# Copying the row numbers of a scatter before the waits for its data, in a mixture-of-experts kernel

## The chip, the cores and the metric
The kernel runs on 1 core of one Trainium2 chip. The metric is device time in microseconds (us) of one execution; smaller is better. Times inside a profile are counted from the first instruction of the profiled execution.

## The reference
Two residual stages over x, 4 x 512 tokens of 512 numbers. The first adds a gated mix of a sigmoid of two rank-one scores and the normalised x. The second adds a gated mixture of experts over the normalised result: every token goes through a shared expert and through its 4 best of 16 experts, with weights packed as 4-bit codes.
```
x = x + tanh(g_xattn) * (0.6 * sigmoid(si + sj + b) + 0.4 * layernorm(x))
h = layernorm(x)
probs = softmax(h @ gate_w.T);  vals, idx = top_k(probs, 4);  w = vals / sum(vals)
y_e = (silu(h @ G_e) * (h @ U_e)) @ D_e          # expert e, weights dequantised
out = sum over the 4 chosen e of w_e * y_e  +  shared expert(h)
x = x + tanh(g_ffn) * out
```

## The kernel before
**Stages.** The first stage, the gating and the shared expert over 16 tiles of 128 tokens come first. The normalised rows are stored to a DRAM table `token_rows`, and x with the shared expert's part is stored to `out`. From about 195 us on the routed part runs: the tokens of each expert are listed in slots of 128 (`tok` holds the row numbers, one column for a slot; short slots are filled with a dump row). In this data there are 72 slots, numbered 0 to 71, and each expert has one slot or more.

**One slot.** POOL (GpSimd) gathers the 128 rows by an indirect DMA into `xg` (line 504); PE transposes them (line 1236), does gate and up (line 1196, in two halves), transposes the activations (line 1210) and does the down product (line 1224); ACT and DVE do the work between. ACT copies the product to `y_sb` (line 640, `mix_room` in the rows) and raises `yev_done`. POOL then adds the 128 rows into `out` by an indirect DMA with an add (line 524), the scatter, and each landed scatter raises `added[b]` by 16. There are two buffers, b = 0 and 1, taken in turn. In slot s PE does the gate and up of s and the down product of s - 1. While that goes on, DVE dequantises the next expert's weights, which SP's queue loads.

**POOL's queue.** It holds, in program order, `gather(s + 4)` and `add(s)` for each slot. The last four adds (68 to 71) have no gathers between them, and are written out behind the loop. An indirect DMA takes its row numbers from a small tile: `idx_g` for gathers and `idx_s` for scatters, each with a column for each buffer, filled by a copy of one column of `tok`. `hold_wait()` (line 493, `pool_tick` in the rows) is a small multiply on POOL that carries the wait ahead of the DMA instruction.

**The waits of a scatter.** A read-add-write of the same row by two scatters must not overlap. Slots of one expert hold different tokens, slots of different experts may hold the same. `added[b] >= 8 * (s - b)` says that scatter s - 2, the last of this buffer, has landed. `others_i` holds for the first slot of an expert the count of `added[1 - b]` that says that all earlier scatters of the other buffer have landed, and 16 for all other slots; POOL's sequencer loads it into a register from SBUF (line 516). The last scatter waits for all before it (line 519). `st_out` says that the plain stores to `out` have landed (line 520).

Of the kernel before, what the change touches and what calls it, by code (L numbers as in the profile page):

```python
# [29 lines left out]
def gated_xattn_moe(nc, x, ctx_512, g_xattn, g_ffn, xattn_w, xattn_b, gate_w, gu_packed, gu_scales,  # L30
                    dn_packed, dn_scales, sh_gu_packed, sh_gu_scales, sh_dn_packed, sh_dn_scales, out):
    B, S, H = x.shape
# [32 lines left out]
    with ExitStack() as ctx:  # L65
        def sb(name, shape, dt):
            return ctx.enter_context(nc.sbuf_tensor(name, shape, dt))
# [4 lines left out]
        def sem(name):  # L72
            return ctx.enter_context(nc.semaphore(name))
# [87 lines left out]
        def in_room_b(shape, dt):  # L161

            n = math.prod(shape[1:])
            piece = room_b[:, at[0]:at[0] + n]
            at[0] += n
            assert at[0] <= B * S
            if dt != F32:
                piece = piece.bitcast(dt)
            return piece.rearrange("p (a b) -> p a b", a=shape[1]) if len(shape) == 3 else piece
        tok = in_room_b([P, SLOTS], I32)  # L170
# [35 lines left out]
        idx_s = sb("idx_s", [P, 2], I32)  # L206
# [64 lines left out]
        st_out = sem("st_out")  # L271
# [16 lines left out]
        yev_done = sem("yev_done")  # L288
        added = [sem("added0"), sem("added1")]
        idx_g_ready = sem("idx_g_ready")  # L290
        idx_s_ready = sem("idx_s_ready")
# [110 lines left out]
        def _(pool):  # L402
# [88 lines left out]
            def hold_wait():  # L491

                nc.gpsimd.tensor_tensor(pool_tick[:, :], ones[:, 0:1], ones[:, 0:1], ALU.mult)
# [12 lines left out]

            def add(s, b, all_before=False):

                pool.wait_ge(yev_done, s + 1)
                if not isinstance(s, int) or s >= 2:  # L510
                    pool.wait_ge(added[b], 8 * (s - b))
                if isinstance(s, int):
                    if s >= 1:
                        pool.wait_ge(added[1 - b], 8 * (s + b))
                else:
                    others = pool.value_load(others_i[0:1, bass.ds(s, 1)], min_val=16, max_val=8 * SLOTS)
                    pool.wait_ge(added[1 - b], others)
                if all_before:
                    pool.wait_ge(added[1 - b], 8 * (s + b))
                pool.wait_ge(st_out, 16 * (B + 1))  # L520
                nc.gpsimd.tensor_copy(idx_s[:, b:b + 1], tok[:, bass.ds(s, 1)]).then_inc(idx_s_ready, 1)  # L521
                pool.wait_ge(idx_s_ready, s + 1)
                hold_wait()
                nc.gpsimd.indirect_dma_start(out[:, :], bass.IndirectOffsetOnAxis(idx_s[:, b:b + 1], 0), y_sb[:, b, :],  # L524
                                             None, compute_op=ALU.add).then_inc(added[b], 16)
            for s in range(4):
                gather(s, s % 2)
            for b in range(2):
                gather(b + 4, b)
                add(b, b)  # L530
            with pool.Fori(2, inner + 1) as j:
                for b in range(2):
                    gather(2 * j + b + 2, b)
                    add(2 * j + b - 2, b)
            for k in range(-4, 0):
                add(2 * inner + 4 + k, k % 2, all_before=k == -1)
# [819 lines left out]
```

## Time and profile before
| | |
|---|---|
| time, median of 3 runs | 717.2 us (716.89 to 717.4) |
| profiled execution, its own time | 715.78 us |
| its span, first to last instruction | 714.1 us |
| mean granted TensorE clock | 0.953 of full speed |
| PE busy (matmul) | 87% of the span |
| DVE, ACT, POOL busy | 69%, 46%, 45% |

The engines are PE (TensorE matmul), PEld (its weight loads), DVE (VectorE), ACT (ScalarE), POOL (GpSimd) and SP (SyncE). An engine's name with a q (POOLq) is its instruction sequencer, which resolves waits and registers ahead of the engine. "Issue" is time in which an engine waited for nothing that the profile shows. A releaser is what ended an idle time; where an instruction had several waits, the one that came last is named.

### The profile page before, as it was taken

How to read it: one execution, taken by the hardware profiler on the slowest of the kernel's cores; microseconds unless marked ns; L12 is line 12 of the kernel's file. 1: busy time of each engine (PE TensorE's matmuls, PEld its weight loads, DVE VectorE, ACT ScalarE, POOL GpSimd, SP SyncE). 2: the span in 40 equal slices, each digit the busy share in tenths (PEclk: the TensorE clock that was granted, in tenths of full speed). 3: DMA queues.
4: the chain of work that ended last, by engine and by line, in shares of the span. 5: the costliest groups of instructions: out<-in, count | busy, mean ns of one | idle time of the engine just before them, and what ended most of it. 6: DMA issues, size and time to landing. Idle time of an engine off the chain costs nothing.

```text
span 714.1 us, 17257 instructions
## 1 busy us (share of the span) xinstructions
PE 620.8 (87%) x4394; PEld 374.8 (52%) x4395; DVE 490.2 (69%) x1271; ACT 325.8 (46%) x558; POOL 324.8 (45%) x506
## 2 busy tenths in 40 slices
PE   3347459995979899999999999999999999999991
PEld 2234236653545456656556566565565556566550
DVE  4695847889857576758778758578678787867110
ACT  1751347632234355455445455454554544554541
POOL 1620354200032456556465475554655646665532
PEclk9759788999899999999999999999999999999997
DMA  6940011204627668584785886758576686754532
GB/s 222 294 139 0 16 45 74 75 1 85 232 53 204 156 143 211 97 210 86 184 187 118 192 175 136 178 106 201 119 180 149 141 204 132 165 88 85 86 40 38
DMA packets 49841, 93.72 MB, mean 131 GB/s; under 512 B 8840, under 2 KB 16776, under 8 KB 49816
## 3 DMA queue, kind: packets, MB, share of 16 engines
q0 software_dynamic: 16128, 38.35, 28.8%
q1 hardware_dynamic: 29464, 49.83, 24.3%
q10 hardware_dynamic: 4224, 5.24, 2.2%
q8 instruction: 11, 0.18, 0.1%
q14 instruction: 14, 0.11, 0.1%
HBM read 65.16 MB, written 28.24 MB: 131 GB/s over the span
## 4 chain that ended last, share of the span: by engine, by line
PE 69%; DVE 13%; DMA 6%; issue 4%; SPq 2%; ACT 2%; POOL 1%; DVEq 1%; POOLq 0%; ACTq 0%
PE gu_ps L1196 41%; PE bank L1224 19%; PE bank L1236 4%; PE bank L1210 4%; DMA dn_sc<-dn_scale_halves 3%; DVE act L987 1%; DMA dn_scale_halves<-wgu 1%; ACT acth L616 1%; DVE stats L721 1%; DVE X L996 1%; DVE mix_room L1023 1%; DVE X L751 1%; PE bank L1180 1%; DVE acth L992 1%; DVE wgu L923 1%
## 5 line engine op out<-in xcount | busy, mean ns | idle before, releaser
L1196 PE MATMUL gu_ps<-wgu,mix_room 128*128 x1728 | 305.4, 327 | 2.4 <-DVE tick L946 1.3
L1196 PEld LDWEIGHTS gu_ps<-wgu,mix_room 128*128 128x128 f16 x1728 | 166.3, 98 | 114.3 <-issue 8.6
L1224 PE MATMUL bank<-wdn,aT 128*128 (+1 forms) x792 | 187.2, 382 | 12.1 <-ACT aT L623 11.5
L623 ACT ACTIVATE aT<-bank 128x768 f16<-128x768 f16 x88 | 71.2, 810 | 130.5 <-PE bank L1210 130.5
L524 POOL DMA_INDIRECT out<-mix_room,idx_s x72 | 121.6, 1689 | 18.5 <-issue 17.9
L1224 PEld LDWEIGHTS bank<-wdn,aT 128*128 128x128 f16 x792 | 77.7, 98 | 97.8 <-ACT aT L623 7.8
L987 DVE SCALAR_TENSOR_TENSOR act<-gu_ps,wslot,sg x72 | 44.5, 618 | 104.5 <-ACT sg L609 91.4
L616 ACT ACTIVATE acth<-act 128x384 f16<-128x384 f32 x88 | 46.0, 523 | 133.0 <-DVE act L987 128.3
L521 POOL COPY idx_s<-room_b 128x1 int32 (+1 forms) x72 | 19.0, 263 | 180.9 <-DMA out<-mix_room,idx_s 117.6
L501 POOL COPY idx_g<-room_b 128x1 int32 (+1 forms) x72 | 58.5, 813 | 75.7 <-DVE tick L857 62.6
L504 POOL DMA_INDIRECT room_b<-token_rows,idx_g x72 | 78.5, 1090 | 10.8 <-issue 1.0
L1196 PE MATMUL gu_ps<-wgu,xT 128*128 128x384 f16 x384 | 72.7, 344 | 5.6 <-DVE tick L980 5.6
L992 DVE TENSOR_TENSOR acth<-act,acth (+1 forms) x88 | 49.5, 563 | 39.6 <-ACT acth L616 38.4
L634 ACT ACTIVATE mix_room<-bank 128x1024 f16<-128x1024 f16 x72 | 73.2, 1017 | 0.5 <-PE bank L1236 0.5
L923 DVE TENSOR_TENSOR wgu<-dq_code,gu_sc 128x768 f16<-128x768 f16 x136 | 71.7, 569 | 2.4
L609 ACT ACTIVATE sg<-gu_ps 128x384 f32<-128x384 f32 x88 | 43.2, 491 | 65.6 <-PE gu_ps L1196 62.0
L1210 PE MATMUL bank<-id,acth 128*128 128x128 f16 x528 | 44.1, 220 | 13.3 <-ACT acth L616 9.3
L1196 PEld LDWEIGHTS gu_ps<-wgu,xT 128*128 128x128 f16 x384 | 38.0, 103 | 31.4 <-issue 11.5
L1210 PEld LDWEIGHTS bank<-id,acth 128*128 128x128 f16 x528 | 36.2, 98 | 27.5 <-ACT acth L616 16.6
L1236 PE MATMUL bank<-id,room_b 128*128 128x128 f16 x576 | 44.4, 220 | 2.8 <-DMA room_b<-token_rows,idx_g 2.8
L929 DVE TENSOR_TENSOR wdn<-dn_code,dn_sc 128x384 f16<-128x384 f16 x136 | 42.9, 357 | 0.7
L640 ACT ACTIVATE mix_room<-bank 128x512 f32<-128x512 f32 x72 | 41.8, 580 | 3.0 <-PE bank L1224 3.0
(161 smaller groups left out, 581.5 us busy)
## 6 DMA issues: line engine op xcount, KB each, us to landing
dn_sc<-dn_scale_halves SPq DMA_DIRECT2D x34, 384.0 KB
dn_raw<-in_L_ffn_down_packed SPq DMA_DIRECT2D x48, 256.0 KB
gu_sc<-gu_scale_halves SPq DMA_DIRECT2D x34, 192.0 KB
X<-in_x ACTq DMA_DIRECT2D x4, 1024.0 KB, 9.6
token_rows<-room_a SPq DMA_DIRECT2D x16, 256.0 KB, 2.0
out<-X SPq DMA_DIRECT2D x4, 1024.0 KB, 11.3
gu_raw<-in_L_ffn_gate_up_packed SPq DMA_DIRECT2D x16, 192.0 KB
gu_raw<-in_L_ffn_gate_up_packed SPq DMA_DIRECT2D x16, 191.9 KB
```

The source lines that it names most:

```text
L501: nc.gpsimd.tensor_copy(idx_g[:, b:b + 1], tok[:, bass.ds(s, 1)]).then_inc(idx_g_ready, 1)
L504: nc.gpsimd.indirect_dma_start(xg[:, b, :], None, rows_dram[:, :], bass.IndirectOffsetOnAxis(idx_g[:, b:b + 1], 0)).then_inc(xg_ld[b], 16)
L524: nc.gpsimd.indirect_dma_start(out[:, :], bass.IndirectOffsetOnAxis(idx_s[:, b:b + 1], 0), y_sb[:, b, :], None, compute_op=ALU.add).then_i ...
L616: nc.scalar.activation(acth[:, b, 0, :], act[:, b, :], ACT.Copy).then_inc(ah_done, 1)
L623: nc.scalar.activation(aT[:, b].rearrange("p a c t -> p (a c t)"), at_ps, ACT.Copy).then_inc(aT_done, 1)
L634: nc.scalar.activation(xTs[:, b, :], xT_ps, ACT.Copy).then_inc(xTs_done, 1)
L923: link(nc.vector.tensor_tensor(wgu[:, buf, hl, c, :], dq_code[:, :], gu_sc[:, buf, hl, :], ALU.mult), wait=False)
L992: nc.vector.tensor_tensor(acth[:, b, 1, :], act[:, b, :], acth[:, b, 0, :], ALU.subtract).then_inc(al_done, 1)
L1196: mm = nc.tensor.matmul(ps[b][:, 0:I], x(xp * HC + c), wgu[:, w, wp, c, col:col + I], start=(c == 0 and xp == 0 and wp == 0), stop=(c == H ...
L1210: mm = nc.tensor.transpose(at_ps[:, k * P:(k + 1) * P], acth[:, b, hl, t * P:(t + 1) * P], id16[:, :])
L1224: mm = nc.tensor.matmul(y_ps[0 if shared else b][:, :], aT[:, b, ap, t, :], wdn[:, w, wp, t, :], start=(n == 0), stop=(n == 3 * IC - 1))
L1236: mm = nc.tensor.transpose(xT_ps[:, k * P:(k + 1) * P], chunk_h(halves[:, k // HC, :], k % HC), id16[:, :])
```

## The change
In `add`, the copy of the row numbers into `idx_s` and the wait for that copy move up. They now stand behind two waits only: that the plain stores have landed, and that the last scatter of the same buffer has landed. The waits for other experts' scatters, with the register load of `others_i`, come behind the copy, and the wait for the result, `yev_done`, which stood first, comes last.
```diff
             def add(s, b, all_before=False):
 
-                pool.wait_ge(yev_done, s + 1)
+                pool.wait_ge(st_out, 16 * (B + 1))
                 if not isinstance(s, int) or s >= 2:
                     pool.wait_ge(added[b], 8 * (s - b))
+                nc.gpsimd.tensor_copy(idx_s[:, b:b + 1], tok[:, bass.ds(s, 1)]).then_inc(idx_s_ready, 1)
+                pool.wait_ge(idx_s_ready, s + 1)
                 if isinstance(s, int):
                     if s >= 1:
                         pool.wait_ge(added[1 - b], 8 * (s + b))
...
                     pool.wait_ge(added[1 - b], others)
                 if all_before:
                     pool.wait_ge(added[1 - b], 8 * (s + b))
-                pool.wait_ge(st_out, 16 * (B + 1))
-                nc.gpsimd.tensor_copy(idx_s[:, b:b + 1], tok[:, bass.ds(s, 1)]).then_inc(idx_s_ready, 1)
-                pool.wait_ge(idx_s_ready, s + 1)
+                pool.wait_ge(yev_done, s + 1)
                 hold_wait()
                 nc.gpsimd.indirect_dma_start(out[:, :], bass.IndirectOffsetOnAxis(idx_s[:, b:b + 1], 0), y_sb[:, b, :],
                                              None, compute_op=ALU.add).then_inc(added[b], 16)
```

## Rows read from the trace of the kernel before
**Rows 1.** The page's head and its engine table: busy us, share, instructions.
```profile
span 714.1 us, 17257 instructions
PE 620.8 (87%) x4394; PEld 374.8 (52%) x4395; DVE 490.2 (69%) x1271; ACT 325.8 (46%) x558; POOL 324.8 (45%) x506
```
**Rows 2.** Busy time by stretches of 50 us, two of the routed part.
```profile
core 0: us, PE busy (x) PEld busy (x) DVE busy (x) ACT busy (x) POOL busy (x), PEclk, DMA share, GB/s
590.00:640.00 50.00, 50.00 (x361) 30.34 (x359) 37.44 (x95) 24.68 (x45) 31.35 (x51) 1.00 0.64 134
640.00:690.00 50.00, 50.00 (x351) 30.01 (x349) 20.18 (x49) 25.27 (x46) 24.90 (x40) 1.00 0.45 74
```
**Rows 3.** The list of waits, POOL's for scatters: total us, times, longest.
```profile
POOL idx_s L521 <- DMA out<-mix_room,idx_s: 117.6, 41, 6.0
POOL idx_s L521 <- ACT mix_room L640: 49.8, 18, 4.3
```
**Rows 4.** The chain that ended last, its end: start us, us, what.
```profile
696.56 0.59 ACT mix_room L640
...
697.18 0.04 POOLq L511
...
697.32 0.29 POOLq L516
...
698.10 0.19 POOL idx_s L521
...
698.36 0.19 POOL pool_tick L493
...
698.80 4.81 DMA out<-mix_room,idx_s
...
703.78 0.19 POOL idx_s L521
...
704.05 0.19 POOL pool_tick L493
...
704.49 1.57 POOL out L524
```
**Rows 5.** The timeline near the end: start us, us, engine, line, operation [idle before].
```profile
692.97 1.57 POOL L524 DMA_INDIRECT out<-mix_room,idx_s  x1 [0.60 <-issue]
...
696.84 0.56 DVE L992 TENSOR_TENSOR acth<-act,acth  x1 [0.73 <-ACT acth L616]
...
701.18 0.60 ACT L640 ACTIVATE mix_room<-bank 128x512 f32<-128x512 f32 x1 [2.35 <-PE bank L1224]
```
**Rows 6.** The wait behind the last scatter: sequencer instruction, ns, first and last start.
```profile
L538 POOLq EVENT_SEMAPHORE  x1: 17/17/17, 709.4 to 709.4; - x1
```
**Rows 7.** The timeline at 275 us, DVE and POOL.
```profile
275.40 0.56 DVE L909 TENSOR_TENSOR dq_mag<-dq_mag,dq_sign 128x768 uint16<-128x768 uint16 x1
275.45 0.55 POOL L521 COPY idx_s<-room_b 128x1 int32 x1 [2.40 <-DMA out<-mix_room,idx_s]
```
**Rows 8.** Scatters' time on POOL, 230 to 680 us, then 685 on: ns min/median/max.
```profile
L524 POOL DMA_INDIRECT out<-mix_room,idx_s x67: 1600/1642/2000, 235.8 to 679.4; - x67
...
L524 POOL DMA_INDIRECT out<-mix_room,idx_s x4: 1573/1574/1585, 686.0 to 704.5; - x4
```
**Rows 9.** The timeline at the first scatters, and the 10 us by the stretches' view.
```profile
225.89 1.64 POOL L524 DMA_INDIRECT out<-mix_room,idx_s  x1 [0.35 <-ACT wslot L630]
...
235.06 0.18 POOL L521 COPY idx_s<-room_b 128x1 int32<-128x1 int32 x1 [5.87 <-issue]
...
235.60 2.11 PE L1196 MATMUL gu_ps<-wgu,mix_room 128*128 x12
235.81 1.60 POOL L524 DMA_INDIRECT out<-mix_room,idx_s  x1 [0.29 <-issue]
...
238.11 0.56 DVE L941 COPY gu_half<-gu_raw 128x768 uint16<-128x768 uint16 x1 [4.46 <-DMA dn_sc<-dn_scale_halves]
...
240.87 0.80 PE L1210 MATMUL bank<-id,acth 128*128 128x128 f16 x6 [3.15 <-ACT acth L616]
...
242.31 3.07 PE L1196 MATMUL gu_ps<-wgu,mix_room 128*128 x12
...
235.00:245.00 10.00, 6.85 (x41) 4.22 (x40) 5.56 (x14) 2.84 (x5) 6.27 (x12) 0.83 0.44 95
```

## The prediction

> **What bounds the kernel now.** The page's engine table comes first: PE is the engine to watch, and POOL, whose queue the change touches, is busy less than half of the span [rows 1]. An average over the span says little, so the table by stretches comes next: in each 50 us of the routed part PE is busy for all of it, at full clock, in the two stretches shown [rows 2]. There a slot takes what its matmuls take; a scatter that leaves a little sooner has no engine on that path to release. The list of waits shows POOL idle for 117.6 us ahead of the row-number copy until an earlier scatter had landed and for 49.8 us until ACT had written the result [rows 3]. That is large, but it is idle time of an engine that does not bound those stretches. Nobody on the path waits for it except where the kernel ends.
>
> So the chain that ended last, read at its end, is the main view [rows 4]. With 72 slots, numbered 0 to 71, the scatters of slots 70 and 71 are the last two. The result of 70 is in SBUF at 697.15 (696.56 + 0.59). POOL's sequencer wakes 0.03 later, loads the register for "other experts' scatters" (the load itself 0.29), gets to the copy at 698.10, to the small holding multiply at 698.36, to the scatter at 698.80. That scatter takes 4.81 us to land, and the last one, which must wait for it, goes copy 703.78, multiply 704.05, scatter 704.49. The result of 71 has been ready since 701.78 (701.18 + 0.60) [rows 5], so the last scatter waits for a landing, not for arithmetic. It lands at 709.4, where the wait after the last scatter passes [rows 6]. From 709.4 to the span's end is 4.7 us that the change does not touch.
>
> **The change, part by part.** It removes and adds no instruction; per scatter it moves the copy, its semaphore wait and, because that now precedes them, lets the load of `others_i` run before the wait for the result. All waits of one scatter still have to pass before it leaves, and nothing else of POOL's queue stands between them, so no new wait is queued before a gather. What matters is only how much sits between the last wait to pass and the scatter.
>
> *Scatter 70, released by the result.* Before: 697.15 to 698.80 is 1.65 us, as 0.95 to the copy, 0.26 copy to multiply, 0.44 multiply to scatter [rows 4]. After: the copy waits only for scatter 68 and the load can be done while POOL idles, so from 697.15 there are the release and the multiply's dispatch, then the same 0.44. For the release I have two neighbours: copy end to multiply start was 0.07 (698.29 to 698.36) and landing to copy start, with a register step between, was 0.16 (703.62 to 703.78). I take 0.10. That gives 0.54 and a saving of 1.11; with the two ends 1.05 to 1.14.
>
> *Does something block the multiply there?* In its new place, near 697.25 instead of 698.36, the multiply falls on a DVE subtraction with two SBUF operands, 696.84 to 697.40 [rows 5]. Such a meeting stands elsewhere in the trace: a copy on POOL that began at 275.45, inside a two-operand DVE instruction of 275.40 to 275.96, took 0.55 rather than 0.18 and ended 0.04 after DVE's end [rows 7]. By that, the multiply would end at 697.44, which is where 697.25 + 0.19 ends anyway: price 0. At the worst it begins only when DVE ends, 697.40 instead of 697.25: 0.15 is the other end. The Trainium skill, "SBUF — State Buffer", section "🔬 SBUF: two separate sides", says that of a GpSimd instruction and a VectorE instruction with two SBUF inputs whichever comes second waits for the shared port pair until the first is through; by it taken strictly the sum would be 0.15 smaller, and the row stands nearer to 0.
>
> *The copy of 71 beside scatter 70.* It now runs while POOL still makes scatter 70's descriptors. The four last scatters, which nothing followed, took 1.573 to 1.585 us on POOL; the 67 before them, from 235.8 on and mostly with a gather's copy behind, had a median of 1.642 and at most 2.000 [rows 8]. So 0.07 more till scatter 70 lands, between 0 and 0.42.
>
> *Scatter 71, released by the landing of 70.* Before, landing to scatter was 0.87 (703.62 to 704.49) [rows 4]. After, only the multiply is left, plus one register step for the result's wait: about 0.14 + 0.44 = 0.58. Saving 0.29; between 0.27 (exactly the copy and its wait) and 0.36 (release 0.07). Its own flight is the 4.9 us that it was (704.49 to 709.4).
>
> The result of 71, 701.78, doesn't take over: scatter 70 would leave at 697.69 and land at 697.69 + 4.81 + 0.07 = 702.57, still 0.8 later. The Trainium skill, "DMA: Bandwidth & Descriptors", section "🔬 Anatomy of one DMA — SWDGE (gpsimd) path", fits a POOL-issued DMA as 2.0 us plus its bytes at 436 GB/s, which for 256 KB is an estimate of 2.6 us. By it scatter 70 would land before the result of 71 both before and after, and only 0.95 + 0.26 less 0.10 of the last scatter, 1.11 us in all, would be saved; the trace has 4.81, and the sum goes by that.
>
> *The middle.* Scatters 2 to 69 leave 0.3 to 1.1 us earlier. The cover is PE's full 50.00 of 50 [rows 2]. Gathers, queued behind scatters, leave earlier too, and nobody waits longer. So 0.
>
> *The start of the routed part.* Scatter 0 at 225.89 follows the landing of the big output stores; there the copy is still behind that wait: 0. Scatter 1 was released by scatter 0's landing, copy 235.06, scatter 235.81 [rows 9]; it will leave 0.27 earlier. Just then DVE stands 4.46 us for a scale load that landed at 238.02, and PE idles 3.15 us after it [rows 9]. Scatter 1's traffic overlaps the last of that load 0.27 longer; if the two halve the bandwidth, the load and everything after come 0.14 later; if the packets were already queued, 0. I take 0.05, nearer to 0 because POOL needs over a microsecond to make the descriptors.
>
> Sum: 1.11 - 0.07 + 0.29 - 0.05 = 1.28 us, against a profiled execution of 715.78 us (span 714.1 and 1.68 around it): 714.5. That execution lies 1.4 below the median of the three runs, 717.2; the saving taken from the median gives **715.9 us**, 0.18% less. With all ends together the saving is 1.05 - 0.15 - 0.42 + 0.27 - 0.14 = 0.6 at the poorest and 1.14 + 0.36 = 1.5 at the best.
>
> **The rivals.**
> 1. *Only the copy is saved, not the register load* (the load or an instruction fetch still ends up behind the result's wait, or scatter 69 lands last for 70). Against it: the load is behind no wait that the result's wait precedes in the new order. For it: the idle time before scatters is irregular, and scatter 69 left at 692.97 [rows 5], so by the same 4.81 it landed at 697.78, just as POOL reached that wait; but it too will leave earlier. Then 2 x 0.27 = 0.54: 716.7 us.
> 2. *More than the sum:* scatter 70 lands so early that the last scatter is bound by the result of 71. Then it leaves at 701.78 + 0.54 = 702.3 instead of 704.49, a saving of 2.2: 715.0 us. It needs scatter 70 to land 0.8 us sooner than reckoned, in under 4.1 us; the quiet queue of the end already gave 4.81.
> 3. *No change:* the end after 709.4 absorbs it, or the middle gives it back. For it: the load near 238 shows that small shifts of transfers reach PE. 717.2 us.
> 4. *Slower: a weight load comes late because a scatter and a gather now leave before it.* Place: the expert change, as near 238 us. One such wait costs PE its 3.15 us idle and 0.96 more on the next twelve matmuls (3.07 against 2.11, at a granted clock of 0.83 in that 10 us stretch) [rows 9], 4.1 us in all. It decides once the shift of some load exceeds its slack; one late load gives 717.2 + 4.1 - 1.3 = 720.0 us. Against it: DVE waited for that kind of load only once in the routed part, and the shift is under 1.1 us.
> A gain in every slot (72 times 0.27 and more, some 20 us) is excluded by rows 2.
>
> **How the numbers follow.** A measurement of this kernel can tell about 0.2% (1.4 us) from no change. The sum's case has 0.58, its own range 715.7 to 716.6; since the point where it counts as faster, 715.77, is only 0.1 from the forecast and the three runs lie 0.5 apart, I give 0.26 of it to faster and 0.32 to same. Rival 1 has 0.14 (same), rival 2 has 0.10 (faster), rival 3 has 0.12 (0.10 same, 0.02 slower by scatter of the runs), rival 4 has 0.06 (0.05 slower, 0.01 same). Faster 0.36, same 0.57, slower 0.07. The range 715.1 to 717.3 leaves out rival 4 and the outer parts of rivals 2 and 3.
>
> **What would show it.** In the profile after: the row-number copy right behind the gather's descriptors, or beside the scatter's; from ACT's end of slot 70 to the scatter 0.5 to 0.6 us instead of 1.65, and no register load between; from that landing to the last scatter under 0.65 instead of 0.87; scatter 70 about 1.1 and the final landing about 1.3 earlier relative to PE's last matmul; PE 50.00 of 50 in the late stretches as before. Wrong would be: a load of `others_i` after ACT's end, PE's last matmul shifted by more than 0.3 us, a multiply of 0.3 us or more on the path, or the last scatter starting with ACT rather than a landing.

## The result, and the profile after

The changed kernel took 713.1 us against 717.3 us for the kernel before (medians of four runs each): ratio 0.9945, 95% interval 0.9929 to 0.9961. By that ratio it is faster by 3.9 us, where 1.3 were forecast, and the time lies 2.0 us below the range. A second comparison (e5 below) gave 0.9950, 0.9932 to 0.9968.

The profiled execution took 713.32 us. The head of its page and its engine table, beside [rows 1]:

```profile
span 711.6 us, 17257 instructions
PE 629.2 (88%) x4394; PEld 379.7 (53%) x4395; DVE 494.9 (70%) x1271; ACT 325.8 (46%) x558; POOL 323.6 (45%) x506
```

The instructions are as many as before; only their order on POOL differs. The timeline of the changed kernel near its end, beside [rows 4, 5] (in this file the copy is line 512):

```profile
695.39 0.58 ACT L640 ACTIVATE mix_room<-bank 128x512 f32<-128x512 f32 x1
...
696.12 0.19 POOL L493 TENSOR_TENSOR pool_tick<-ones 128x1 f32<-128x1 f32 x1 [3.31 <-ACT mix_room L640]
...
696.77 1.57 POOL L524 DMA_INDIRECT out<-mix_room,idx_s  x1 [0.46 <-issue]
696.85 0.81 ACT L623 ACTIVATE aT<-bank 128x768 f16<-128x768 f16 x1 [0.88 <-PE bank L1210]
697.78 0.77 POOL L512 COPY idx_s<-room_b 128x1 int32 x1
...
700.01 0.60 ACT L640 ACTIVATE mix_room<-bank 128x512 f32<-128x512 f32 x1 [2.35 <-PE bank L1224]
701.59 0.19 POOL L493 TENSOR_TENSOR pool_tick<-ones 128x1 f32<-128x1 f32 x1 [3.04 <-DMA out<-mix_room,idx_s]
701.93 1.58 POOL L524 DMA_INDIRECT out<-mix_room,idx_s  x1 [0.15 <-issue]
```

The result of slot 70 is there at 695.97 (695.39 + 0.58), its scatter leaves at 696.77, 0.80 later instead of 1.65. The row numbers of 71 are copied beside scatter 70, and the last scatter waits only for the landing. So the end is as the prediction drew it, and worth about what it said. To set the ends side by side I count from ACT's last copy of the transposed activations (`aT`, one in each slot): 696.85 here; in the kernel before it is the second of these rows of its timeline:

```profile
262.90 0.81 ACT L623 ACTIVATE aT<-bank 128x768 f16<-128x768 f16 x1 [1.57 <-PE bank L1210]
...
698.03 0.81 ACT L623 ACTIVATE aT<-bank 128x768 f16<-128x768 f16 x1 [0.88 <-PE bank L1210]
```

From it to the last scatter are 6.46 us before (704.49 - 698.03) and 5.08 after (701.93 - 696.85); to the end of the span 16.0 and 14.7. That is **the tail**: 1.3 us gained. The first row opens what I call **the loop part**, 65 slots, from 262.90 to 698.03: 435.1 us. The time of a slot is counted from one such copy to the next; most take 6.55 or 6.70 us. "The slot into expert 5" is the first slot of expert 5. The same row in the timeline of the changed kernel:

```profile
264.03 0.81 ACT L623 ACTIVATE aT<-bank 128x768 f16<-128x768 f16 x1 [1.57 <-PE bank L1210]
```

From 264.03 to 696.85 are 432.8 us: **2.3 us gained in the stretch for which the prediction had said 0.** Loop part and tail make 3.6 us together. The spans of the two profiles differ by 2.5 only, because the routed part began 1.1 us later in the changed kernel's profile. That start lies anywhere between 262.5 and 265.2 us in the fourteen profiles of this study, in either order of POOL's instructions, so it is not put down to the change. The prediction had shown two stretches in which PE is busy for 50.00 of 50 us. Four others of the kernel before, in the same view as [rows 2], are these:

```profile
340.00:390.00 50.00, 48.43 (x342) 28.96 (x340) 39.99 (x100) 24.32 (x44) 27.14 (x43) 1.00 0.73 166
390.00:440.00 50.00, 49.18 (x356) 29.85 (x355) 36.52 (x93) 25.08 (x45) 27.89 (x45) 1.00 0.77 175
...
490.00:540.00 50.00, 49.32 (x358) 29.96 (x356) 37.28 (x94) 25.62 (x47) 28.41 (x46) 1.00 0.73 166
540.00:590.00 50.00, 48.97 (x341) 28.99 (x340) 39.32 (x101) 24.32 (x44) 25.76 (x41) 1.00 0.71 167
```

PE lacks 1.57, 0.82, 0.68 and 1.03 us in them, 4.1 in all, at full clock (column PEclk 1.00). PE's timeline of the kernel before shows where: six pauses, all in front of the transposes of the activations, 27 to 94 us apart (shown are those of half a microsecond or more from 300 us to the last slot).

```profile
342.86 0.49 PE L1210 MATMUL bank<-id,acth 128*128 128x128 f16 x6 [0.69 <-issue]
370.39 0.50 PE L1210 MATMUL bank<-id,acth 128*128 128x128 f16 x6 [0.88 <-ACT acth L616]
397.87 0.49 PE L1210 MATMUL bank<-id,acth 128*128 128x128 f16 x6 [0.82 <-ACT acth L616]
491.71 0.49 PE L1210 MATMUL bank<-id,acth 128*128 128x128 f16 x6 [0.68 <-issue]
552.13 0.49 PE L1210 MATMUL bank<-id,acth 128*128 128x128 f16 x6 [0.53 <-issue]
579.43 0.49 PE L1210 MATMUL bank<-id,acth 128*128 128x128 f16 x6 [0.50 <-issue]
```

The same timeline of the changed kernel has three left:

```profile
343.64 0.49 PE L1210 MATMUL bank<-id,acth 128*128 128x128 f16 x6 [0.50 <-issue]
397.74 0.49 PE L1210 MATMUL bank<-id,acth 128*128 128x128 f16 x6 [0.80 <-ACT acth L616]
578.05 0.49 PE L1210 MATMUL bank<-id,acth 128*128 128x128 f16 x6 [0.76 <-issue]
```

Each pause stands at an expert change behind an expert of four slots. There DVE has the longest chain between two activations: the low halves (line 992), the last dequantising steps of the next expert, the signal to SP, the first dequantising steps of the expert behind, and a load of the next expert's first slot and slot count into registers (line 1095); only then can it begin the activation (line 987) that PE's transposes need. The pause at 370.39 hangs on the activation at 368.37, the first of expert 5. Its load, the scatter before it and the activation itself, in the kernel before. First the sequencer's load, from the view of its line (ns three times, then first and last start), then the timeline:

```profile
L1095 DVEq TENSOR_LOAD <-first_tiles_i x1: 952/952/952, 366.3 to 366.3; - x1
```

and around it:

```profile
363.65 1.80 POOL L524 DMA_INDIRECT out<-mix_room,idx_s  x1 [0.30 <-issue]
...
364.50 0.62 DVE L894 TENSOR_SCALAR dq_mag<-gu_half 128x768 uint16<-128x768 uint16 x1
...
368.37 0.62 DVE L987 SCALAR_TENSOR_TENSOR act<-gu_ps,wslot,sg  x1 [1.20 <-issue]
```

In the changed kernel, at the same expert change, the view of the line:

```profile
L1095 DVEq TENSOR_LOAD <-first_tiles_i x1: 301/301/301, 366.8 to 366.8; - x1
```

and around it:

```profile
363.55 1.62 POOL L524 DMA_INDIRECT out<-mix_room,idx_s  x1 [0.51 <-issue]
...
365.28 0.35 DVE L894 TENSOR_SCALAR dq_mag<-gu_half 128x768 uint16<-128x768 uint16 x1
...
368.23 0.62 DVE L987 SCALAR_TENSOR_TENSOR act<-gu_ps,wslot,sg  x1 [0.55 <-issue]
```

The load took 0.95 us, now 0.30, and DVE's pause ahead of the activation went from 1.20 to 0.55 "issue": time that no list of waits puts down to anybody. What differs is where the load falls against the scatter: 2.60 us after its start before (366.25 less 363.65), 3.21 after (366.76 less 363.55).

The load is not all of it. The instruction of line 894 began 0.85 us after the scatter in the kernel before and took 0.62 us; in the changed kernel it stands 1.73 us after it and took 0.35. So from the activation before to this one DVE needed 8.10 us, and now 7.19: 0.65 less for the load and 0.26 less for line 894. At experts 9 and 11 it is the same pair (8.10 and 7.98 to 7.18 and 7.19). All six expert changes with a pause in the kernel before have both, a load of 0.42 to 0.95 us and line 893 or 894 stretched by 0.26.

From here the theory, called A below and G once the times were known: in the loop the new order gains nothing by scatters that land sooner. It moves POOL's scatter against DVE's chain, out of a place where it holds up a load of DVE's sequencer, and stretches a DVE instruction; G names the load alone.

### The profile page after: what moved, and what is told of

Same layout as the page of the kernel before. It is cut to its first block, busy times and chain, and to the rows that moved or that the text cites. A ratio compares the mean times of both kernels' runs of the same rounds, so it can differ in the third digit from the quotient of the medians.

```text
span 711.6 us, 17257 instructions
## 1 busy us (share of the span) xinstructions
PE 629.2 (88%) x4394; PEld 379.7 (53%) x4395; DVE 494.9 (70%) x1271; ACT 325.8 (46%) x558; POOL 323.6 (45%) x506
## 4 chain that ended last, share of the span: by engine, by line
PE 73%; DVE 12%; DMA 5%; issue 3%; ACT 2%; SPq 2%; POOL 1%; DVEq 0%; POOLq 0%; ACTq 0%
PE gu_ps L1196 43%; PE bank L1224 21%; PE bank L1236 4%; PE bank L1210 4%; DMA dn_sc<-dn_scale_halves 3%; DVE act L987 1%; DVE stats L721 1%; ACT acth L616 1%; DMA dn_scale_halves<-wgu 1%; DVE X L996 1%; DVE mix_room L1023 1%; PE bank L1180 1%; DVE wgu L923 1%; DVE acth L992 1%; DVE room_a L1020 1%
## 5 line engine op out<-in xcount | busy, mean ns | idle before, releaser
L1224 PE MATMUL bank<-wdn,aT 128*128 (+1 forms) x792 | 189.3, 385 | 11.7 <-ACT aT L623 11.1
L493 POOL TENSOR_TENSOR pool_tick<-ones 128x1 f32<-128x1 f32 x144 | 35.5, 246 | 163.7 <-DMA out<-mix_room,idx_s 84.9
L504 POOL DMA_INDIRECT room_b<-token_rows,idx_g x72 | 76.5, 1062 | 12.3 <-issue 3.8
L1196 PE MATMUL gu_ps<-wgu,xT 128*128 128x384 f16 x384 | 74.4, 350 | 5.3 <-DVE tick L980 5.3
L501 POOL COPY idx_g<-room_b 128x1 int32 (+1 forms) x72 | 40.1, 558 | 80.1 <-DVE tick L857 62.6
```

Of the source, the lines that this page charges most:

```text
L504: nc.gpsimd.indirect_dma_start(xg[:, b, :], None, rows_dram[:, :], bass.IndirectOffsetOnAxis(idx_g[:, b:b + 1], 0)).then_inc(xg_ld[b], 16)
L1196: mm = nc.tensor.matmul(ps[b][:, 0:I], x(xp * HC + c), wgu[:, w, wp, c, col:col + I], start=(c == 0 and xp == 0 and wp == 0), stop=(c == H ...
L1224: mm = nc.tensor.matmul(y_ps[0 if shared else b][:, :], aT[:, b, ap, t, :], wdn[:, w, wp, t, :], start=(n == 0), stop=(n == 3 * IC - 1))
```

## The experiments

Loop part and tail are read from each kernel's profile, as above; ratios are to the kernel before, run beside them. The kernel before had medians of 715.8 to 716.6 us in the comparisons from e1 to e12, so the ratios count, not the times. A ratio is that of the record, with its interval; it is not the quotient of the medians and differs from it by up to 0.001 (e3: medians 712.1 and 715.8). In the first rows "changed" is the first comparison, e5 the second of the same kernel.

| kernel | ratio (95%) | loop part | tail |
|---|---|---|---|
| before | 1 | 435.1 | 16.0 |
| changed | 0.9945 (0.9929 to 0.9961) | 432.8 | 14.7 |
| e1_tail_only | 0.9992 (0.9983 to 1.0002) | 434.8 | 15.3 |
| e2_loop_only | 0.9970 (0.9958 to 0.9983) | 433.6 | 15.8 |
| e3_after_later | 0.9959 (0.9945 to 0.9973) | 432.5 | 14.4 |
| e4_before_load_early | 0.9968 (0.9957 to 0.9979) | 433.0 | 16.0 |
| e5_after_again | 0.9950 (0.9932 to 0.9968) | 432.8 | 14.7 |
| e6_after_load_early | 0.9944 (0.9923 to 0.9965) | 432.8 | 14.4 |
| e7_later_load_early | 0.9940 (0.9922 to 0.9959) | 433.2 | 14.6 |
| e8_before_gather_later | 0.9994 (0.9982 to 1.0006) | 435.1 | 15.6 |
| e9_one_multiply | 0.9966 (0.9952 to 0.9979) | 433.3 | 15.7 |
| e10_two_multiplies | 0.9957 (0.9943 to 0.9970) | 433.1 | 14.5 |
| e11_all_loads_early | 0.9924 (0.9910 to 0.9937) | 430.5 | 14.6 |
| e12_before_all_early | 0.9938 (0.9916 to 0.9960) | 430.2 | 16.3 |

**Either part alone (e1, e2, e5).** `add_late` is `add` in the old order, `add_early` in the new.
```diff
 # e1: the tail's scatters in the new order (e2: the other way round)
-                add(b, b)
+                add_late(b, b)
...
-                    add(2 * j + b - 2, b)
+                    add_late(2 * j + b - 2, b)
...
-                add(2 * inner + 4 + k, k % 2, all_before=k == -1)
+                add_early(2 * inner + 4 + k, k % 2, all_before=k == -1)
```


> The new order only for the last four scatters (68 to 71); all earlier ones keep the old order. Theory A (two parts: the tail gives 1.3 us because two scatters in a row leave sooner; the rest of the gain comes in the loop, because POOL's gathers and scatters fall at other moments of DVE's chain at expert changes): 1.3 us faster than before, about 716.0, and the slots with 7.4 to 7.6 us at expert changes stay as they were before. Rival B (the whole gain of some 4 us comes from the end of the kernel, and the rest of the profile's difference is chance): about 713.1. Rival C (the gain comes only if all scatters are moved): 717.3.

> The new order for scatters 0 to 67, the old order for the last four. Theory A: between 1.2 us (what the profiles show between the first routed slot and PE's last product, 2.4, less what went the other way before) and 2.9 us (the measured 4.2 less 1.3) faster than before, 714.4 to 716.1; fewer slots at expert changes over 7.2 us. Rival B: 717.3, no change. Theory A and B also differ in the tail: from PE's last product to the end 13.0 us as before.

> The changed kernel once more, beside the others of this study. In the first four experiments the kernel before had 715.8 us; the tail alone gave a ratio of 0.9992 and the loop alone 0.9970. If the two parts add (theory A), the changed kernel has a ratio of 0.9962, about 713.1 against 715.8. If there is a third part that needs both, or the first comparison (0.9945) was right as it stood, 0.9945 or less.

The loop gives the larger part: 0.9970, with a loop part 1.6 us shorter in its profile and the old tail, so that B (all in the tail) and C (only both together) fall. The tail alone gave 0.6 us (-0.1 to 1.2), less than the 1.3 expected. Its profile shows one way in which that comes about, at its end:

```profile
697.22 1.57 POOL L543 DMA_INDIRECT out<-mix_room,idx_s  x1 [0.46 <-issue]
...
698.32 3.62 PE L1243 MATMUL bank<-wdn,aT 128*128 x9 [1.05 <-ACT aT L642]
701.97 0.60 ACT L659 ACTIVATE mix_room<-bank 128x512 f32<-128x512 f32 x1 [3.85 <-PE bank L1243]
702.72 0.19 POOL L493 TENSOR_TENSOR pool_tick<-ones 128x1 f32<-128x1 f32 x1 [3.71 <-ACT mix_room L659]
703.37 1.57 POOL L543 DMA_INDIRECT out<-mix_room,idx_s  x1 [0.46 <-issue]
```

PE's last product took 3.62 us instead of 2.11: the granted clock was 0.83 in the 10 us from 695, the lower level (1.2 GHz) for part of them, after PE had paused 1.05 us for the copy of activations behind other short pauses. So the result of slot 71 came at 702.57, and the last scatter waited for ACT and not for the landing. From the last `aT` copy to it are then 6.06 us (703.37 - 697.31), against 5.08 in the changed kernel and 6.46 before: 0.4 gained instead of 1.4. The changed kernel's PE paused as long there (1.04 us) and then took 2.11, so the pause alone does not decide it; what does stays open. Three of the fourteen profiles had the slow product (e1, e9, e12); the old order hides it behind the landing (e12's last scatter still waits for the DMA), the new one does not. The two parts multiply to 0.9962 against the 0.9945 and 0.9950 of the whole. The intervals are wide enough for this to be chance. The profiles show one part of it: e2 has the loop's order of the changed kernel, but in its profile the load into expert 5 began 2.53 us after the scatter and took 0.96 (slot 7.50), where both profiles of the changed kernel have 0.30 (slot 6.55). Why the same order falls out differently there is not settled.

**More work on POOL between the result and the scatter (e3, e9, e10).** Each multiply is some 0.19 us with 0.08 between; e9 has one more in the loop, e10 two, e3 three.
```diff
                 pool.wait_ge(yev_done, s + 1)
                 hold_wait()
+                for k in range(later):
+                    nc.gpsimd.tensor_tensor(pool_late[:, k:k + 1], ones[:, 0:1], ones[:, 0:1], ALU.mult)
...
-                    add(2 * j + b - 2, b)
+                    add(2 * j + b - 2, b, later=3)             # e9: 1, e10: 2
```


> The changed kernel, with three more small multiplies (some 0.27 us each) on POOL between the wait for the result and the scatter in the loop, so that scatters and the gathers behind them leave about 0.8 us later, near where they left before the change; copy and register load stay early. Theory A (what matters in the loop is at which moment POOL works beside DVE): most of the loop's gain is lost, 714.5 to 716.0, and the slow expert changes are back. Rival D (the early copy itself helps, the moment of the scatter does not matter): 713.1, as the changed kernel.

> The changed kernel with one more multiply (0.27 us) on POOL before each scatter of the loop (e3_after_later had three). Theory G, out of the traces so far: a load by DVE's sequencer that begins 2.4 to 3.2 us after a scatter began on POOL ends only some 3.5 us after that scatter; all others take 0.30 to 0.32. In the changed kernel the loads into experts 5, 9 and 11 begin 3.21 us after the scatter; now 2.94: they take 0.5 to 0.6 us, and these three slots grow by 0.3 to 0.6 each. 0.7 to 1.5 us slower than the changed kernel: ratio 0.996 to 0.997. Rival H (what counts is only that the scatters leave early or late, in proportion): 0.1 to 0.3 us slower than the changed kernel.

> The same with two more multiplies (0.54 us). Theory G: the loads into experts 5, 9 and 11 begin 2.67 us after the scatter and take 0.8 to 0.9 us, as in the kernel before; these slots are back at 7.2 to 7.5 us, only the tail's gain is left: ratio 0.997 to 0.9985, slower than with three multiplies (0.9959). Rival H: between the changed kernel (0.995) and e3_after_later (0.9959).

Two of the three missed the theory's numbers (A in e3, G in e10): they came out faster. That of e9, 0.9966, lies in its range, but not for the reason given: the loads into experts 9 and 11 stayed short. And e10's 0.9957 lies where rival H had put it. Three more multiplies cost nothing that can be seen (0.9959, loop part 432.5), where the loop's gain should have gone. One reason shows in the profile of e9: in the changed kernel the scatter stands about 0.5 us of "issue" behind the multiply (median of the loop 0.50, in e9 0.24), and one more multiply fills that pause instead of adding to it. The loads into experts 9 and 11 so began 3.18 and 3.19 us after the scatter and not 2.94, and stayed at 0.30. Where POOL did come out later (expert 5 in e9: load 2.51 us after the scatter, 0.68 us long) the slot was back at 7.23 from 6.55. And with three multiplies the scatter is so late that most loads stand ahead of the place that matters (1.5 and 1.9 us after it, 0.30 long). Its slots into experts 6 and 12 still took 7.34 and 7.18 us with loads of 0.31 and 0.32: at even experts, where a new round of DVE's loop over pairs begins, DVE's pause ahead of the activation is 1.0 us even with a short load, and 0.55 at odd ones. A held load is thus not the only thing that makes such a slot long. So "later is as before" was wrong as a reckoning. That the places decide, not how early a scatter leaves, stands: H, a cost in proportion, would have e3 the slowest of the three, and its loop part is the shortest.

**Gathers later, in the kernel before (e8).**
```diff
                 hold_wait()
+                for k in range(later):                     # 3 in the loop
+                    nc.gpsimd.tensor_tensor(pool_late[:, k:k + 1], ones[:, 0:1], ones[:, 0:1], ALU.mult)
                 nc.gpsimd.indirect_dma_start(xg[:, b, :], None, rows_dram[:, :],
```


> The kernel before, with three more multiplies (0.8 us in all) on POOL between a loop gather's copy and its indirect DMA; scatters keep their order and waits. Nothing on PE's path waits for a gather. Theory A (DVE's load of the expert's count is slow when a gather's descriptors begin within 0.4 us of it, at experts 1, 4, 5, 6, 9, 11, 12): the gather now begins 0.8 us later, the load falls in front of it and takes 0.3 us again, while the 0.30 us that DVE loses beside the scatter stays: 1 to 3 us faster than before, although POOL only got more work, ratio 0.996 to 0.9985. Rival F (more work on POOL can only cost): 1.000 or slower.

Ratio 0.9994, and the loads as slow as ever. The load at the same expert change (its line is 1098 here), by the view of its line:

```profile
L1098 DVEq TENSOR_LOAD <-first_tiles_i x1: 967/967/967, 368.5 to 368.5; - x1
```

POOL's timeline around it:

```profile
366.10 1.62 POOL L527 DMA_INDIRECT out<-mix_room,idx_s  x1 [0.15 <-issue]
367.16 0.84 POOL L502 COPY idx_g<-room_b 128x1 int32 x1
...
368.37 1.12 POOL L506 TENSOR_TENSOR pool_late<-ones 128x1 f32<-128x1 f32 x3
369.64 1.03 POOL L507 DMA_INDIRECT room_b<-token_rows,idx_g  x1
```

The gather now begins a microsecond behind the load's start and the load takes 0.97 all the same, 2.42 us after the scatter. The gain that theory A gave for this run did not come. That clears the gather, which I had suspected, and leaves the scatter. Over all fourteen profiles, of 210 such loads since the first scatter, the 36 that began 2.37 to 3.06 us after the start of a scatter on POOL took 0.49 to 1.12 us and ended 3.19 to 3.62 us after it; none of the other 174 took more than 0.45, nearly all 0.30 to 0.32. The rule was read out of the profiles up to e8, then with 2.4 to 3.2 us. Of the later runs only e9 and e10 have loads in the narrower window, four, and these took 0.53 to 0.68; their loads at 3.08 to 3.19 took 0.30 to 0.32, so the upper bound was set afterwards. e11 and e12 have no load in it: they test what the loads are worth, not the window.

**The load early on DVE (e4, e6, e7, e11, e12).** POOL as it is, before (e4, e12) or changed (e6, e11; e7 with e3's multiplies). The program hands no register from one round of DVE's loop over pairs to the next, so e4 reaches odd experts, e6 and e7 even ones, and e11 and e12 have the loop written out for all.
```diff
+                following = tiles_of(e + 1) if load_next else None
                 if not isinstance(e, int) or e < E - 2:
                     dequant(n + 1, 1 - buf_next, 0, None)
+                return following
...
 # e11, e12
-            with v.Fori(1, E // 2 - 1) as h:
-                expert(2 * h, 0)
-                expert(2 * h + 1, 1)
+            for e in range(1, E - 1):
+                following = expert(e, e % 2, loaded_=following, load_next=True)
...
```


> The kernel before, POOL untouched. On DVE the load of an expert's first slot and slot count is made one step earlier for experts 1, 3, 5, ... 15: ahead of the first dequantising steps of the weights behind, instead of right before the expert's first activation. Theory A (PE loses 0.7 to 0.9 us at an expert change because DVE's chain of 13 instructions with that load, 6.6 to 6.8 us, is longer than a slot allows): at experts 1, 5, 9 and 11, whose load took 0.84 to 1.11 us, the slot loses most of its excess, 1.5 to 3 us in all: 714.3 to 715.8. Rival E (the long load is a symptom, DVE's chain has slack there): 717.3.

> The changed kernel with DVE's load of first slot and count made earlier for experts 2, 4, ... 14 and 15 (DVE's loop turned by one expert, so that the load stands ahead of the first dequantising steps). Theory A: in the profile of the changed kernel the slow expert changes left are those into experts 4, 6 and 12 (slots of 7.20, 7.51 and 7.62 us against 6.55 to 6.70), with loads of 0.32, 0.54 and 0.53 us; they shrink by 0.3 to 0.8 each: 0.8 to 2 us faster than the changed kernel, ratio 0.993 to 0.995 to the kernel before. Rival E (the DVE chain has slack): no better than the changed kernel.

> The third experiment's kernel (three more multiplies on POOL before a loop scatter) with the same earlier load on DVE. That kernel had a ratio of 0.9959 and slow expert changes of 7.04, 6.88, 7.34, 7.14 and 7.18 us at experts 4, 5, 6, 11 and 12. Theory A: those into 4, 6 and 12 shrink by 0.3 each at least: ratio 0.994 to 0.995. If what decides is only where POOL's instructions fall, and the load is short there anyway (0.30 to 0.32 us), no gain beyond 0.9959.

> The changed kernel with DVE's loop over expert pairs written out, so that the load for every expert, odd and even, stands ahead of the dequantising steps before its first activation. POOL is as in the changed kernel. Theory G: no load lies in DVE's chain any more at any expert change; the slots into experts 4, 6 and 12 (7.20, 7.51, 7.62) shrink by 0.3 to 0.8 and no other grows: ratio 0.992 to 0.994, the fastest of all. Against it: the written-out code is more than twice as long on DVE, and if its instructions arrive late at taken branches, that costs a microsecond or more: 0.996 and above.

> The kernel before (old order on POOL everywhere) with the DVE loop written out and all its loads early, as in e11_all_loads_early (ratio 0.9924, loop part 430.5 us in its profile). Theory G says that the new order gains in the loop only through those loads: here the loop part is 430.5 to 431.5 us although POOL's order is the old one, and what is missing against 0.9924 is the tail, 0.6 to 1.3 us: ratio 0.993 to 0.9945. Rival D (the new order has a loop gain of its own, some 2 us): loop part 432.5 to 433.5, ratio 0.996 to 0.9975.

e4, without a touch to POOL, gives 0.9968, as much as the new order in the loop alone: the slots into experts 5, 9 and 11 go from 7.59, 7.39 and 7.50 us to 6.65, 6.59 and 6.84. The earlier load also moves the instructions behind it, and the stretched one of line 893 or 894 is back at 0.36 at all three; e4 does not part the two. e6 mends experts 4, 6 and 12 (7.20, 7.51 and 7.62 to 6.86, 6.65 and 7.00) and worsens 5, 9 and 11 (7.52, 6.97 and 7.25): with the loop turned by one expert, the load of expert 5 stands 2.95 us after the scatter and takes 0.56, and experts 9 and 11 now begin a round of the loop, with pauses of 0.97 us behind loads of 0.31. Its ratio, 0.9944, lies in the range written down, but beside the changed kernel (0.9945 and 0.9950, the same loop part) there is no gain, where 0.8 to 2 us were expected. e7 is alike: 0.9940 lies in its range, its loop part, 433.2, is no shorter than e3's 432.5. With all loads early, e11 is the fastest kernel of the study: 0.9924. PE's timeline from 300 us to the last slot has no pause of half a microsecond or more left in it; this is the load at the expert change shown above, in e11 by the view of its line:

```profile
L1095 DVEq TENSOR_LOAD <-first_tiles_i x1: 300/300/300, 363.6 to 363.6; - x1
```

and in e12:

```profile
L1095 DVEq TENSOR_LOAD <-first_tiles_i x1: 304/304/304, 363.9 to 363.9; - x1
```

e12 decides between G and D. With the loads early and the old order on POOL, the loop part is 430.2 us, as short as e11's 430.5. Once the loads are early at every expert change, the new order has no gain left in the loop. What it gained there it gained in DVE's chain at those changes, and at experts 5, 9 and 11, where most of it lies, 1.84 of the 2.6 us by which the chains got shorter are the loads and 0.79 the stretched instruction. No run was made that changes one of the two and leaves the other. What is left of the new order is the tail: 0.9938 against 0.9924, with intervals that overlap.

## Why the prediction was wrong

**What bounds the kernel.** That PE bounds the loop was right, and that POOL's long waits release nobody too. What was wrong was to read two full stretches as all. The same view, asked for the whole loop, has 4.1 us of missing PE time in four other stretches; the list of waits, which puts short pauses down to several names, did not make up for that.

**Scatter 70.** Forecast 0.54 us from result to scatter, measured 0.80 (695.97 to 696.77): 0.85 saved instead of 1.11. The release was 0.15, not 0.10, and from the multiply to the scatter it took 0.65 instead of 0.44: the pause behind the multiply, 0.46 instead of 0.25, now holds POOL's register steps for the copy of 71.

**The multiply beside DVE.** It began at 696.12, inside DVE's subtraction (695.66 to 696.22), and took 0.19: price 0, as the row had it. The rule weighed there (the Trainium skill, "SBUF — State Buffer", section "🔬 SBUF: two separate sides"), taken strictly, would have had it begin at 696.22, 0.10 later; this meeting does not bear it out in that form.

**The copy of 71 beside scatter 70.** It took 0.77 us beside the scatter, and the scatter's 1.57 us on POOL did not grow: 0 instead of 0.07.

**Scatter 71.** From landing to scatter 0.4 instead of 0.58: 0.46 saved instead of 0.29. From the multiply to the scatter it was 0.34 and not 0.44. With these, the tail's sum, forecast 1.33, was 1.3. The right sum is luck in part: it came of misses that cancel, 0.26 too much for scatter 70, 0.17 too little for scatter 71, and 0.07 for a delay that did not come. Rival 2's bound, the result of slot 71, does bind, but from the other side: not because scatter 70 lands early, but because PE's last product ran at the low clock for part of its time in some profiles (e1, e9), one of the signs of being wrong that the prediction had named. Timed alone the tail gave 0.6 us.

**The middle: the step that failed.** The forecast missed by its term for the middle, 0, where 2.3 us were measured. "So 0" had two parts. The cover, PE's full 50 of 50, was not there at the expert changes. And "nobody waits longer" asked only who waits for POOL's instructions, not what they hold up while they run. What ran beside them was held up: DVE's register load, and a DVE instruction beside the scatter. The slots into experts 4, 5, 9 and 11 took 7.39, 7.59, 7.39 and 7.50 us before and 7.20, 6.55, 6.55 and 6.84 after, 2.7 us less; all other slots of the loop part together took 0.4 more. The timed difference is 3.9 us, 0.3 more than loop part and tail of the profiles; that is not settled, and the profiled execution before was itself 1.4 us under its median.

**The start.** The scale load near 238 us kept DVE waiting 4.42 us (before: 4.46), so that no run shows the 0.05. Rival 4 (a weight load comes late) did not come about; rival 1 neither, since no register load stands between ACT's end of slot 70 and its scatter.

## What to carry to other kernels

Before calling a stretch covered by a busy engine, ask for every stretch of it, and follow the pauses of even half a microsecond that come back at the same point of an outer loop. An instruction moved on a slack engine can gain or lose by what it runs beside, above all register loads of another engine's sequencer; "issue" ahead of an instruction is the place to look. And where a load can stand ahead of work that does not need it, put it there: done at every expert change (e12) that gave as much as the reordering. Done at half of them it can give nothing, because it moves the others too (e6).

## What the runs showed of the hardware

- A load of a register from SBUF by DVE's sequencer takes 0.30 to 0.32 us in the loop (the first of each execution, ahead of all scatters, 0.55), but it was held in all 36 cases in which it began 2.37 to 3.06 us after a scatter of 128 rows of 2 KB began on POOL: it took 0.49 to 1.12 us, until 3.2 to 3.6 us after that start. A gather's start does not do this (e8). That it is the scatter's transfer, and at which port, is argued only. The Trainium skill, "DMA: Bandwidth & Descriptors", section "🔬 Latency and other measured facts", gives `tensor_load` a floor of about 600 ns; the loads here took half of that.
- Beside a scatter some DVE instructions are stretched. In the changed kernel, of 80 that began 0.55 to 0.95 us after a scatter's start on POOL, 28 took 0.2 to 0.3 us more than their kind does; line 915 took 0.65 instead of 0.36 at 277.17, and 0.36 in 19 others of its starts in that window. What decides is not shown.
- A scatter of 256 KB with an add lands 4.8 us after its start on POOL with the queue quiet [rows 4], and the same after the change. The 2.6 us of the fit weighed in the prediction do not hold for it.
- PE's last nine matmuls took 2.11 us in eleven profiles and 3.4 to 3.6 in three, with the same instructions of PE ahead of them; in e1 the granted clock was 0.83 in that stretch of 10 us.
